# Turning the row maxima of a two-layer graph network back with transposes of 128 rows

## The reference, cut to what matters

```
# layer 0, run twice (W1, then W2), h = relu(layernorm(x)), then the first output through relu
xk  = einsum('ni,kio->nko', x, W)            # 25 matrices of 64 x 64, on a 5 x 5 spline grid
msg = sum over 4 corners of basis * xk[src, idx]
agg = segment_max(msg, dst); agg = 0 where a node has no edge
out = agg + x @ root + bias
# layer 1, h = relu(layernorm(x))
d      = two-layer MLP of edge_attr_3 (gelu, layer norm)
logits = (h@W1)[dst] - (h@W2)[src] + d
a      = softmax of logits within each dst
out    = segment_sum(a * ((h@W3)[src] + d), dst)
```

## Time and profile before

| | us |
|---|---|
| median of 3 runs | 2384.97 |
| lowest, highest | 2373.78, 2391.5 |
| span of the profiled execution, first to last instruction | 1831.4 |
| busy in the span: PE, DVE, POOL, ACT | 1524.8, 1481.5, 1228.0, 732.2 |

### The profile page before, as it was taken

The page is one execution under the profiler, slowest core; times in us unless marked ns, Lnnn a source line. Parts: engine busy times, 40 slices in busy tenths (PEclk is TensorE's granted clock), DMA queues, the critical chain, the costliest instruction groups (busy, mean ns, idle before and its releaser), DMA issues.

```text
span 1831.4 us, 33936 instructions
## 1 busy us (share of the span) xinstructions
PE 1524.8 (83%) x7745; PEld 989.1 (54%) x7745; DVE 1481.5 (81%) x2831; ACT 732.2 (40%) x1841; POOL 1228.0 (67%) x1207
## 2 busy tenths in 40 slices
PE   2977888888888986999999999997777767667764
PEld 1264566566656665777777777775443334334432
DVE  3688999999999985999999999986777667666664
ACT  2463333333333323323322333223655545554553
POOL 4004777777777757777777777751577777777776
PEclk8588999999999997999999999998999999998998
DMA  5993444444444534887777777773233332333230
GB/s 99 164 110 65 101 104 107 100 106 101 106 105 101 106 73 124 242 233 231 228 225 221 227 227 226 233 221 88 60 80 67 80 67 68 69 77 69 67 73 19
DMA packets 408085, 232.10 MB, mean 127 GB/s; under 512 B 305989, under 2 KB 381958, under 8 KB 408046
## 3 DMA queue, kind: packets, MB, share of 16 engines
q1 hardware_dynamic: 311730, 151.97, 31.2%
q0 software_dynamic: 44864, 65.52, 16.4%
q10 hardware_dynamic: 51452, 14.18, 6.1%
HBM read 141.71 MB, written 92.64 MB: 128 GB/s over the span
## 4 chain that ended last, share of the span: by engine, by line
PE 34%; POOL 11%; issue 8%; DVE 3%; DMA 3%; ACT 3%; POOLq 0%; DVEq 0%; ACTq 0%; SPq 0%
PE bank L980 17%; POOL gath L581 6%; POOL out_dram L588 6%; PE bank L973 3%; PE bank L1039 2%; PE bank L1022 2%; DMA gath<-M,gidx 2%; PE bank L1101 2%; PE bank L1011 2%; PE bank L1031 1%; PE bank L1000 1%; PE bank L1048 1%; DMA arena<-T 1%; PE bank L1120 1%; DVE arena L1570 1%
## 5 line engine op out<-in xcount | busy, mean ns | idle before, releaser
L980 PE MATMUL bank<-Wk,arena 128*128 128x320 f32 (+1 forms) x2352 | 657.6, 465 | 56.9 <-ACT arena L762 56.9
L980 PEld LDWEIGHTS bank<-Wk,arena 128*128 128x128 f32 (+1 forms) x2352 | 328.0, 189 | 304.6 <-issue 223.3
L581 POOL DMA_INDIRECT gath<-T,gidx x392 | 387.1, 988 | 146.9 <-issue 111.1
L581 POOL DMA_INDIRECT gath<-in_x_dram,gidx x196 | 197.3, 1007 | 161.1 <-ACT gidx L679 102.3
L581 POOL DMA_INDIRECT gath<-M,gidx x196 | 213.5, 1089 | 124.9 <-issue 55.8
L762 ACT ACTIVATE arena<-bank 128x256 f32<-128x256 f32 (+1 forms) x392 | 169.6, 433 | 308.3 <-PE bank L973 307.8
L588 POOL DMA_INDIRECT T<-srow,sidx x196 | 214.6, 1095 | 79.4 <-issue 66.8
L1348 DVE TENSOR_TENSOR arena<-bank,A 128x320 f32<-128x320 f32 x392 | 191.6, 489 | 66.4 <-PE bank L980 59.2
L588 POOL DMA_INDIRECT out_dram<-srow,sidx x196 | 199.8, 1019 | 61.3 <-issue 60.7
L973 PE MATMUL bank<-ident,arena 128*128 128x128 f32 x980 | 171.7, 274 | 10.6 <-DVE arena L1328 10.5
L973 PEld LDWEIGHTS bank<-ident,arena 128*128 128x128 f32 x980 | 124.6, 142 | 41.5 <-issue 7.3
(11 more groups left out here) (185 smaller groups left out, 2738.8 us busy)
## 6 DMA issues: line engine op xcount, KB each, us to landing
arena<-T SPq DMA_DIRECT2D x48, 816.0 KB
T<-arena SPq DMA_DIRECT2D x96, 272.0 KB
T<-zero ACTq DMA_DIRECT2D x1, 13281.2 KB, 103.9
B<-arena SPq DMA_DIRECT2D x49, 256.0 KB
arena<-B SPq DMA_DIRECT2D x49, 256.0 KB, 3.8
arena<-in_x_dram SPq DMA_DIRECT2D x48, 256.0 KB, 4.1
out_dram<-arena SPq DMA_DIRECT2D x48, 256.0 KB, 3.5
begins_cut<-begins_d SPq DMA_DIRECT2D x49, 128.5 KB, 3.5
```

The costliest lines, as they stand in the source:

```text
L581: pool.indirect_dma_start(out=gath[slot][:, j, k, 0:width], out_offset=None, in_=table, in_offset=bass.IndirectOffsetOnAxis(gidx[slot][:, ...
L980: return pe.matmul(bank[2 + r][:, 0:KO], ZT[q][rows, chunk, :], Wk[n - 1][rows, weights].rearrange("p k o -> p (k o)"), start=start, stop= ...
```

## The change

`agg` and `full` are given 128 partitions (`agg_rows`, `full_rows`), of which `agg` and `full` are the lower 64. The scans write the lower half as before. The upper half is zeroed once: four memsets of 128 x 512 in place of one of 64 x 512 and one of 64 x 1. `turn_back` and the turning of `full` now take all 128 partitions, with the whole identity as the moving operand. Each of the four transposes thus writes 128 columns, not 64, and the four fill the bank; the readers take the first 64 of each 128 columns. The order of instructions on every engine is as before, apart from the two memsets more on DVE. Line numbers below the edits move by one to four.

```diff
-        agg = [conv_mem.take([C, EG]) for _ in (0, 1)]
+        agg_rows = [conv_mem.take([P, EG]) for _ in (0, 1)]
+        agg = [t[0:C] for t in agg_rows]
...
-        full = [att_mem.take([C, EG]) for _ in (0, 1)]
+        full_rows = [att_mem.take([P, EG]) for _ in (0, 1)]
+        full = [t[0:C] for t in full_rows]
...
                         act.activation(srow[e.slot(SLOTS)][:, :, 0:C],
-                                       bank[5][:, 0:TPG * C].rearrange("p (t c) -> p t c", c=C), ACT.Copy)\
+                                       bank[5][:, :].rearrange("p (t c) -> p t c", c=P)[:, :, 0:C], ACT.Copy)\
...
                     for j in range(TPG):
-                        tr = pe.transpose(bank[5][:, j * C:j * C + C], agg[e.parity][:, j * P:j * P + P],
-                                          ident[0:C, 0:C])
+                        tr = pe.transpose(bank[5][:, j * P:j * P + P], agg_rows[e.parity][:, j * P:j * P + P],
+                                          ident[:, :])
...
-                        tr = pe.transpose(bank[1][:, j * C:j * C + C], full[e.parity][:, j * P:j * P + P],
-                                          ident[0:C, 0:C])
+                        tr = pe.transpose(bank[1][:, j * P:j * P + P], full_rows[e.parity][:, j * P:j * P + P],
+                                          ident[:, :])
...
-                V_.memset(agg[1], 0.0).then_inc(s_mem, 1)
+                V_.memset(agg_rows[0], 0.0)
+                V_.memset(agg_rows[1], 0.0).then_inc(s_mem, 1)
...
-            V_.memset(full[1][:, EG - 1:EG], 0.0).then_inc(s_mem, 1)
+            V_.memset(full_rows[0], 0.0)
+            V_.memset(full_rows[1], 0.0).then_inc(s_mem, 1)
...
-                V_.tensor_tensor(X[:, :, 0, :], bank[1][:, 0:TPG * C].rearrange("p (t c) -> p t c", c=C),
+                V_.tensor_tensor(X[:, :, 0, :], bank[1][:, :].rearrange("p (t c) -> p t c", c=P)[:, :, 0:C],
                                  b2[g.parity][:, :, C:2 * C], ALU.add).then_inc(at["x1"].sem, 1)
```

## The result

| us | before | after |
|---|---|---|
| median (lowest to highest), 20 runs each | 2393.74 (2368.22 to 2430.83) | 2395.85 (2377.24 to 2426.36) |
| after over before, 95% interval | | 1.0107 [1.0076, 1.0139] |
| profiled execution after: time, span | | 2409.76, 2408.0 |

What follows compares the result with a forecast made beforehand. PE was taken to bound convolution 2, POOL attention and nearly convolution 1. Convolutions -7.1 and -0.5, attention zero, memsets +0.5 and +0.5 made -6.6 us: span 1831.4 to 1824.8, plus 553.6 untouched, predicted 2378 us, range 2362 to 2396.

Steps and rivals of the forecast that it cites:

- the sum: Whole kernel: -7.1 - 0.5 + 0.5 + 0.5 = -6.6 us, taken off the profiled span, with 553.6 us outside it untouched.
- PE alone sets the pace: Convolution 2: PE has no idle time, so 0.15 us less in each of 47 full rounds gives -7.1 us.
- The price on PE: The four transposes and their neighbours on PE: 128 rows throughout take 0.14 to 0.15 us less a round.
- The excesses: Around the 64-row transposes: extra PE time, 0.37 us in all, put down to changes between 64 and 128 rows.
- rival B: Both convolutions: excesses are not of the rows and stay, wider transposes add 0.22 us a round, +21 us, 2407; chance 0.09.
- at all other neighbours in these rows the height stays at 128: Convolution 2 on PE: offered as evidence that row changes cause the excesses, since no such excess stands at those neighbours.
- This second loop: Convolution 1: the loop through POOL's scatters and gathers gains nothing; 0.01 us shorter a round taken, -0.5 us in all.
- POOL's 448 of 450 us: Convolution 1: POOL's busy time plus gaps fill the window, leaving at most 0.05 us a round to gain.
- The forecast of zero: Attention: POOL sets the pace, so PE's saving there brings zero, with -5 us as the far end.
- The memsets: Added DVE zeroing: +0.5 us in `set_up` and +0.5 before attention, together at most +1.5.
- rival C: Convolution 2: no gain, PE's 0.15 us turns into a wait for DVE's sums or the gather; 2386 us, chance 0.08.

Runs made afterwards that it cites:

- after_plain: The changed kernel with every indirect gather of POOL replaced by a plain DMA of the same bytes from consecutive rows; median 1779.81 us.
- before_plain: The kernel before with every indirect gather of POOL made a plain DMA from consecutive rows, run again as base for after_plain; median 1795.94 us.
- plain_gathers: The kernel before with every indirect gather of POOL replaced by a plain DMA from consecutive rows, scatters kept; 1791.48 us, ratio 0.7525.

## Why the prediction was wrong, step by step

**The step that failed** is in the sum: "The profiled span of 1831.4 becomes 1824.8; the 553.6 us that lie between span and median are not touched." They are not work around the program. They are waits inside it, in all three large stages. After against the page of before: 766.9 and 533.1 us from the first to the last transposes of end rows in convolution 2 (the rows below), 681.6 and 507.8 us in attention (L1137 and L1135), and 656 and 517 us from the first to the last turning of messages in convolution 1.

```profile
L1033 PE MATMUL bank<-ident,lnc x100: 272/273/421, 871.6 to 1638.5; 128*128 128x128 f32 x100
```
```profile
L1031 PE MATMUL bank<-ident,lnc x100: 272/273/273, 718.6 to 1251.7; 128*128 128x128 f32 x100
```

**"PE alone sets the pace" of convolution 2** is true of the profiled execution, and -7.1 us is what it is worth where updates are in time (-7.0 measured). In the timed executions PE idles for 98 of 440 us, rounds take 16.1 to 17.0 us, and nothing of the 7 us is seen. That they end in a wait for an update is my reading and not shown; extra work in the same place did lengthen the stage, so PE's time there is not simply hidden.

**The price on PE** was right, wherever one looks. Medians of all turnings of the convolutions at full clock, in the parts of the forecast (ahead, from the first to the fourth, to the next product, its first pitch): narrow 0.206, 0.237, 0.154, 0.373, together 0.97 us; wide 0.112, 0.328, 0.109, 0.272, together 0.82. The excesses are of the rows and go with them; rival B is excluded. The forecast had missed the best evidence for it: "at all other neighbours in these rows the height stays at 128" is not so. Each product pair has two matmuls of 64 rows, in the trace four records, and the first 128-row product behind them takes 0.373 us to its next where the others take 0.269 (medians of 41 rounds of convolution 2 in the page of before). The last 128-row product ahead of them takes 0.362. These 0.10 and 0.09 are the very excesses of the turning, and they stand in the kernels before and after alike. In attention the first pitch of the transposes behind falls from 0.165 to 0.109 as well. That all three excesses vanish together agrees with what the Trainium skill says ("TensorEngine Tiling (Array Packing)", Key Properties): a change of tiling mode drains TensorE. Where the clock stands at its lower level, as in a fifth to somewhat over a third of the turnings of the timed executions, narrow takes 1.66 us and wide 1.50 to 1.60, so the lower clock does not turn the saving round. The row of after that answers to the earlier trace rows, and that of after_plain:

```profile
L1050 PE MATMUL bank<-ident,arena x392: 272/273/448, 171.9 to 1653.3; 128*128 128x128 f32 x196
```
```profile
L1047 PE MATMUL bank<-ident,arena x392: 272/273/301, 172.9 to 1254.9; 128*128 128x128 f32 x196
```

**Convolution 1** rested on a pace that POOL does not set alone: "This second loop closes over two rounds and gains nothing." With plain gathers, which leave POOL far from booked, before's round is still 10.84 us, and the change takes 0.14 off it. So another loop is as long as POOL's 448 of 450 us; an engine can be booked and another loop be just as long. Whether POOL's loop would have held the change back with all indirect DMAs and updates in time is not tested, as no run of the changed kernel had both.

**Attention**: plain gathers shortened its round from 10.61 to 9.66 us, which agrees with POOL having set the pace. The forecast of zero held with plain gathers, but POOL is not booked there, so another loop is the reason.

**The memsets**: not measured apart. From the last end-row transposes to the first L1132 or L1134, before_plain takes 59.4 us and after_plain 61.7, 2.3 more, of which the forecast had 0.5. With -7 and -7 for the convolutions that leaves about -12 of the 16 us. The rest is no gain of the change, as far as the traces show. The profiled execution of before_plain has four long rounds in convolution 1, 13.8 to 15.5 us, where the same program in plain_gathers took 10.8 to 12.5. That makes its convolution 1 11.7 us longer (529.2 against 517.5). Against plain_gathers, 1789.1 us, the span of after_plain, 1776.5, is 12.6 shorter.

**What stays open**: why eight indirect DMAs a step hold updates back, and why one execution, that of the page of before, was free of it. One thing is seen beside it. Where updates are late, the traces also lack records: that of after has some 15,000 records of updates, that of before 37,355, and before_plain's convolution 2 as many a microsecond as before's. The Trainium skill, "NOTIFIC — the notification-queue block", section 7.1, describes a block for such records that holds its senders back when its internal queues are full rather than lose a record; the same section says that its own measurements never saw an overflow. By that the lateness would come from recording what is timed; no run here shows it. And whether the true effect of the change in timed executions is zero or some tenths of a per cent either way is open as well; rival C's condition ("if PE shows idle time in convolution 2") is the one that came, by a mechanism it did not name.

## What to carry to other kernels

Before summing savings along the profiled execution, compare its span with the timed runs. A gap of a quarter is not launch overhead until something shows it; if it lies inside, the profile's bottleneck is not that of the time that counts. A wait whose releaser ended microseconds earlier is a wait for the message. Shortening work beside such waits gained nothing that could be seen here, and lengthening it cost time in one stage and none in another, so read each stage and not the total. And a kernel can be put into the state where a forecast holds, here by plain in place of indirect DMAs, to test a price of 0.15 us in a round to a hundredth.

## What the runs showed of the hardware

- Eight indirect DMAs of 128 rows in a round of 11 us go with updates that arrive late (ACT reads the turned nodes of convolution 2 some 6 us late in the median, 7.7 at most) and rounds 18 to 53% longer (12.73 to 13.87 us in convolution 1 against 10.83, 16.1 to 17.0 in convolution 2 against 11.09); four a round leave them at 10.83 and 11.13. The rows that they fetch do not matter.
- Four transposes of 64 rows between others of 128 take 0.97 us with what they cost their neighbours, of 128 rows 0.82; at the lower clock 1.66 against 1.50 to 1.60. The price stands at each change of rows looked at: about 0.09 us ahead of 64 rows and 0.10 in the first 320-column product behind them, inside each product pair too.
- Extra work on an engine with much idle time is free in one stage and not in another: the fourfold narrow turning lengthened convolution 2 from 762 to 810 us and left attention at 643 against 651 to 698, where the granted clock was 0.88 in place of 0.82. With updates in time the same edit cost 122 us.
